# Mixture-of-experts layer on one core: sums over partitions by TensorE in place of GpSimd, one-hots in pairs of token columns

## The chip, the core and the metric
One core of a Trainium2 chip runs the whole layer as one program. The metric is the device time of one execution in microseconds (us). Engines are TensorE (PE, with PEld for its weight loads), VectorE (DVE), ScalarE (ACT), GpSimd (POOL) and the DMA issuer SyncE (SP). They run side by side, each through its own list of instructions in order, and wait for each other by semaphores.

## The reference
```python
xf = ifft(fft(x.reshape(B,T,4,64), axis=1) * gate, axis=1).real   # gate: one number per channel, so this scales x
x_right = hamilton(xf, conj(normalize(q_right)))                  # quaternion products, linear in x
c = hamilton(normalize(cond), x_right).reshape(B, T, 256)
h = c @ W_in + b_in                                               # "z" below
probs = softmax(h @ W_gate + b_gate)                              # 8 experts
topv, topi = top_k(probs, 2); topv = topv / sum(topv)
mid = relu(einsum('nd,edh->neh', h, W1) + b1)                     # 256 -> 1024, per expert
eout = einsum('neh,ehd->ned', mid, W2) + b2                       # 1024 -> 256
out = x + (sum over the 2 chosen experts of topv * eout) @ W_out + b_out
```
There are 4096 tokens of 256 channels, in float32. Only the two chosen experts of a token have to be worked out.

## The kernel before, in words
**Front.** The 4096 tokens are 32 columns of 128 tokens, handled as 16 pairs. TensorE transposes each pair of x (`x_pair`, L876), ScalarE copies it to `xt_sb` (L477). The whole conditioning and `W_in` are folded into one matrix `weff`, and the gate into `wg`, so that `logits_pair` (L885) and `z_pair` (L895, L898) are plain products of the transposed x. ScalarE copies z out of PSUM (L489) and squares it for its norm (L495), GpSimd stores it to DRAM (`z_by_token`, L397). VectorE picks the two experts of each token, counts tokens per expert, and gives each (token, choice) a slot: experts are put in an order by their counts, and each expert's slots are padded to a multiple of 256. The list "which token sits in which slot" is made by a product of one-hot matrices: VectorE writes `ohb` (row in a tile, 128 x 32 per choice k) and `oha` (tile column, 78 x 32, twice), L749 to L754, and TensorE multiplies them, one matmul for each of the 32 token columns and each k (`rows_of_slots`, L907, 64 matmuls).

**Tiles.** There are `NTILE` = 39 tiles of 256 slots. For tile a, GpSimd gathers its z rows by indirect DMA (`gather`, L428), TensorE transposes them (`rows_t`, L964, called "row transposes of tile a" below), ScalarE and VectorE split them into a high and a low half in float16 (`rows_high` L536, `rows_low` L794), TensorE runs the first layer (L983 to L985, 48 matmuls), ScalarE scales and clips (L549), VectorE splits again (L815, L817), TensorE runs the second layer (L998, 48 matmuls), VectorE finishes y (L805), and GpSimd scatters it (`scatter`, L435). TensorE's order is: first layer of a, row transposes of a+1, second layer of a-1. An expert has at least `GT` = 4 tiles; t = a % 4.

**Weights.** Those of the next expert come in while the current one is worked on. SP loads them (L321, L324), ScalarE squares them with a sum along each partition (L499, L504, in t = 0), GpSimd sums over the partitions (`norms`, L393, in t = 0) to get the norm, VectorE turns it into a power of two (`powers`, L662 to L664, in t = 1), GpSimd works out the scales of that expert (`table`, L411 to L421, in t = 1), and ScalarE and VectorE split the weights in four quarters (`piece`: L511 and L671, two in t = 2 and two in t = 3). A maximum over the partitions (L403) gives the scale of z.

**Order of GpSimd in the tile loop**, by hand:
```python
if a + 2 < NTILE: pool.wait_ge(s_tp, a + 1); gather(a + 2)
if a: scatter(a - 1)
j = a // GT + 1
if j < E and a % GT == 0: norms(j)
if j < E and a % GT == 1: table(j)
```
**End.** After the last tile the two choices of each token are loaded, mixed, transposed and multiplied with `W_out` (L1028, L1038).

## Time and profile before
| what | value |
| --- | --- |
| median of 3 runs | 677.98 us (672.96 to 685.27) |
| profiled execution | 670.79 us, its span 669.1 us |
| PE busy in the span | 578.9 us (87%) |
| DVE, ACT, POOL busy | 360.3, 298.0, 240.7 us |
| mean granted clock of PE | 0.918 of full speed |

The span is the time from the first to the last instruction of the profiled execution. All rows below come from that one execution, so differences are reckoned against its 670.79 us. A clock of 1.00 is TensorE's level of 2.4 GHz, 0.50 its level of 1.2 GHz.

### The profile page before, as it was taken

How to read it: one execution, taken by the hardware profiler on the slowest of the kernel's cores; microseconds unless marked ns; L12 is line 12 of the kernel's file. 1: busy time of each engine (PE TensorE's matmuls, PEld its weight loads, DVE VectorE, ACT ScalarE, POOL GpSimd, SP SyncE). 2: the span in 40 equal slices, each digit the busy share in tenths (PEclk: the TensorE clock that was granted, in tenths of full speed). 3: DMA queues.
4: the chain of work that ended last, by engine and by line, in shares of the span. 5: the costliest groups of instructions: out<-in, count | busy, mean ns of one | idle time of the engine just before them, and what ended most of it. 6: DMA issues, size and time to landing. Idle time of an engine off the chain costs nothing.

```text
span 669.1 us, 14435 instructions
## 1 busy us (share of the span) xinstructions
PE 578.9 (87%) x4527; PEld 493.5 (74%) x4528; DVE 360.3 (54%) x712; ACT 298.0 (45%) x534; POOL 240.7 (36%) x299
## 2 busy tenths in 40 slices
PE   3999993698996997996997898899799999992886
PEld 2996562486895886886886787687689898981665
DVE  5457404346556556556456357357455555542754
ACT  2404533445545555455455365366334343521443
POOL 4003112334345344344434425525524242317700
PEclk9959887789998998999899899899799999996799
DMA  6305215102412412412412402400111111148585
GB/s 189 105 1 206 101 47 181 32 30 98 120 48 88 127 40 93 126 40 90 129 36 82 134 32 87 139 25 32 63 48 49 47 57 40 49 143 280 169 271 189
DMA packets 40355, 64.64 MB, mean 97 GB/s; under 512 B 5943, under 2 KB 28156, under 8 KB 40316
## 3 DMA queue, kind: packets, MB, share of 16 engines
q1 hardware_dynamic: 31548, 39.51, 18.2%
q0 software_dynamic: 8768, 24.65, 11.4%
q8 instruction: 19, 0.31, 0.2%
q14 instruction: 20, 0.16, 0.1%
HBM read 45.53 MB, written 18.61 MB: 96 GB/s over the span
## 4 chain that ended last, share of the span: by engine, by line
PE 49%; issue 21%; POOL 14%; DMA 8%; DVE 4%; ACT 1%; SPq 1%; POOLq 1%; DVEq 0%; ACTq 0%
PE bank L998 19%; PE bank L898 5%; PE bank L983 4%; PE bank L985 4%; PE bank L984 4%; POOL region L428 4%; DMA region<-z_by_token,src 3%; PE bank L885 3%; POOL y_by_choice L435 3%; PE bank L907 3%; PE bank L964 2%; DMA w1s<-y_by_choice 2%; DMA w1s<-in_x 2%; POOL w1s L461 2%; PE bank L1028 1%
## 5 line engine op out<-in xcount | busy, mean ns | idle before, releaser
L549 ACT ACTIVATE region<-bank,b1p,cbits 128x256 f32<-128x256 f32 x312 | 157.0, 561 | 203.2 <-PE bank L985 143.9
L998 PE MATMUL bank<-w2s,region 128*128 x1872 | 218.8, 279 | 0.1
L998 PEld LDWEIGHTS bank<-w2s,region 128*128 128x128 f16 x1872 | 186.6, 100 | 27.0 <-issue 2.0
L983 PE MATMUL bank<-region,w1s 128*128 128x256 f16 x624 | 172.3, 276 | 3.6 <-DVE region L794 3.6
L984 PE MATMUL bank<-region,w1s 128*128 128x256 f16 x624 | 172.1, 276 | 0.0
L985 PE MATMUL bank<-region,w1s 128*128 128x256 f16 x624 | 172.0, 276 | 0.0
L435 POOL DMA_INDIRECT y_by_choice<-region,dst x78 | 80.8, 1036 | 171.3 <-DVE region L805 155.2
L815 DVE CAST region<-region 128x512 f16<-128x512 f32 x156 | 68.5, 439 | 114.3 <-ACT region L549 88.5
L817 DVE TENSOR_TENSOR region<-region 128x512 f16<-128x512 f32 x156 | 108.6, 696 | 5.4
L428 POOL DMA_INDIRECT region<-z_by_token,src x78 | 80.6, 1034 | 23.3 <-issue 22.2
L964 PE MATMUL bank<-ident,region 128*128 128x128 f32 x156 | 27.6, 306 | 50.1 <-DMA region<-z_by_token,src 50.1
L983 PEld LDWEIGHTS bank<-region,w1s 128*128 x624 | 61.8, 99 | 12.0 <-issue 4.2
L985 PEld LDWEIGHTS bank<-region,w1s 128*128 x624 | 61.8, 99 | 7.8
L984 PEld LDWEIGHTS bank<-region,w1s 128*128 x624 | 61.8, 99 | 7.7
L805 DVE SCALAR_TENSOR_TENSOR region<-bank,cbits,b2b 128x256 f32<-128x256 f32 x78 | 34.1, 479 | 48.4 <-PE bank L998 48.4
L964 PEld LDWEIGHTS bank<-ident,region 128*128 128x128 f32 x156 | 20.2, 156 | 53.1 <-DMA region<-z_by_token,src 52.7
L794 DVE SCALAR_TENSOR_TENSOR region<-bank,sx,region 128x512 f16<-128x512 f32 x39 | 29.1, 746 | 41.4 <-ACT region L536 41.4
L536 ACT ACTIVATE region<-bank,sx 128x512 f16<-128x512 f32 x39 | 26.9, 689 | 47.8 <-PE bank L964 29.4
L397 POOL DMA_DIRECT2D z_by_token<-w1s x16 | 12.5, 780 | 80.3 <-ACT w1s L489 80.3
L898 PE MATMUL bank<-w1s,w2s 128*128 128x256 f32 x128 | 37.2, 441 | 0.0
L850 DVE SCALAR_TENSOR_TENSOR w1s<-w1s,route 128x256 f32<-128x256 f32 x32 | 23.1, 766 | 19.2 <-ACT w1s L578 19.2
L898 PEld LDWEIGHTS bank<-w1s,w2s 128*128 128x128 f32 x128 | 26.7, 219 | 8.2 <-issue 4.5
(183 smaller groups left out, 488.0 us busy)
## 6 DMA issues: line engine op xcount, KB each, us to landing
region<-in_L_ffn_W SPq DMA_DIRECT2D x16, 1024.0 KB
w1s<-y_by_choice SPq DMA_DIRECT2D x16, 512.0 KB, 4.3
w1s<-in_x SPq DMA_DIRECT2D x8, 512.0 KB, 7.1
z_by_token<-w1s POOLq DMA_DIRECT2D x16, 256.0 KB, 2.7
w1s<-in_x SPq DMA_DIRECT2D x4, 1024.0 KB
out<-w1s SPq DMA_DIRECT2D x16, 256.0 KB, 2.6
region<-z_by_token,src POOLq DMA_INDIRECT x78
y_by_choice<-region,dst POOLq DMA_INDIRECT x78
```

Of the source, the lines that this page charges most:

```text
L428: g.indirect_dma_start(out=gx[:, a % 2, h, :], out_offset=None, in_=zbuf, in_offset=bass.IndirectOffsetOnAxis(ap=at, axis=0)).then_inc(s_g ...
L435: g.indirect_dma_start(out=ybuf, out_offset=bass.IndirectOffsetOnAxis(ap=at, axis=0), in_=ysb[:, a % 2, h, :], in_offset=None).then_inc(s_ ...
L549: m = s.activation(midf[:, b, c * TS:(c + 1) * TS], FB[b][:, c * TS:(c + 1) * TS], ACT.Relu, bias=b1p[:, bass.ds(r, 1), f:f + 1].rearrange ...
L805: last = v.scalar_tensor_tensor(ysb[:, par, h, :], YB[par][:, h * D:(h + 1) * D], cbits[:, 1, 1, bass.ds(r, 1)].bitcast(f32), b2b[:, bass. ...
L815: v.tensor_copy(mids[:, par, 0, b, :], midf[:, b, :]).then_inc(s_mh, 1)
L817: v.tensor_tensor(mids[:, par, 1, b, :], midf[:, b, :], mids[:, par, 0, b, :], ALU.subtract).then_inc(s_mq, 1)
L898: last = mm(bank[i % 4][:, t * D:(t + 1) * D], xt_sb[:, i, t, k, :], weff[:, k, :], start=False, stop=(k == KD - 1), skip_group_check=True)
L964: last = tr(XB[par][:, k * TS + h * P:k * TS + (h + 1) * P], gx[:, par, h, k * P:(k + 1) * P], ident[:])
L983: mm(o, w, xs[:, par, 0, k, :], start=(k == 0), stop=False)
L984: mm(o, w, xs[:, par, 1, k, :], start=False, stop=False)
L985: last = mm(o, w1_at(e, 1, k, 2 * b + c), xs[:, par, 0, k, :], start=False, stop=(k == KD - 1))
L998: last = mm(YB[par][:, h * D:(h + 1) * D], mids[:, par, l, b, c * TS + h * P:c * TS + (h + 1) * P], w2_at(e, w, f), start=(f == 0 and l == ...
```

## The change
1. The three kinds of sums over partitions leave GpSimd. The sum of squares of the weights becomes a matmul with a matrix of ones (`norms` on PE), after the first layer of each t = 1 tile, written to two columns of a transpose bank; VectorE copies it out in `powers`. The maximum for z becomes a transpose, a reduction on VectorE and a matmul. PE waits for `powers` in t = 2, and for the split weights (`s_wl`) in t = 0 of every expert.
2. The one-hots are laid out as (pair of token columns, entry, column in the pair): entries that a matmul reads one after the other lie 4 bytes apart. Before they lay 64 bytes apart.
3. The PSUM banks of the front are dealt out anew: transposes have two banks (`TB`), logits two (`LB`), z four (`ZB`) of their own. The product of the one-hots goes behind z pairs 8 and 11 (before 10 and 13).
4. ScalarE squares expert 0's weights two pairs earlier, and splits them after all z pairs; VectorE splits them after the exponents (`s_ho`).
5. The loop over experts covers 6 rather than 7 of them, the rest is written out.

```diff
-            def norms(j):
-                pool.wait_ge(s_sq1, j + 1)
-                pool.wait_ge(s_sq2, j + 1)
-                g.partition_all_reduce(wn[:, j, :], wss[:, j, :], P, RADD).then_inc(s_sp, 1)
...
-                if i == 11:
-                    norms(0)
-            pool.wait_ge(s_zn, 1)
-            g.partition_all_reduce(zmax[:, 1:2], zmax[:, 0:1], P, RMAX).then_inc(s_zm, 1)
...
-                if j < E and a % GT == 0:
-                    norms(j)
...
-                if i >= 12:
-                    piece(0, i - 12)
             z_squares(NP - 1)
+            for i in range(4):
+                piece(0, i)
...
+            def powers(j, at):
                 dve.wait_ge(s_sp, j + 1)
+                link(v.tensor_copy(wn[:, j], at))
...
-                v.tensor_tensor(ohb[:, k], iota16[:], bc(slot16[:, 1, k, :].unsqueeze(1), [P, P, NT]),
-                                ALU.is_equal).then_inc(s_ohu, 1)
+                v.tensor_tensor(ohb[:, k], bc(iota16[:].unsqueeze(1), [P, NB, P, 2]),
+                                bc(u.unsqueeze(2), [P, NB, P, 2]), ALU.is_equal).then_inc(s_ohu, 1)
...
-            piece(0, 0)
-            piece(0, 1)
-            piece(0, 2)
             dve.wait_ge(s_zsq, NP)
             v.tensor_reduce(zmax[:, 0:1], zss[:], AX.X, ALU.max).then_inc(s_zn, 1)
-            piece(0, 3)
+            dve.wait_ge(s_zt1, 1)
+            v.tensor_reduce(ztop[:], LB[0][0:1, 0:P], AX.X, ALU.max).then_inc(s_zt2, 1)
             dve.wait_ge(s_zm, 1)
+            link(v.tensor_copy(zmax[:, 1:2], LB[0][:, 0:1]))
...
+            for i in range(4):
+                piece(0, i)
...
-                    last = mm(bank[7][:, 0:2 * NA], ohb[:, k, :, t], oha[:, k, :, :, t],
+                    last = mm(bank[7][:, 0:2 * NA], ohb[:, k, t // 2, :, t % 2], oha[:, k, t // 2, :, :, t % 2],
...
+            def norms(j, at):
+                pe.wait_ge(s_sq1, j + 1)
+                pe.wait_ge(s_sq2, j + 1)
+                mm(at, ones[:], wss[:], start=True, stop=True).then_inc(s_sp, 1)
...
-                if i == 10:
+                if i == 8:
                     rows_of_slots(0)
-                if i == 13:
+                if i == 11:
                     rows_of_slots(1)
+                    norms(0, TB[1][:, 0:2])
+            pe.wait_ge(s_zn, 1)
+            tr(LB[0][0:1, 0:P], zmax[:, 0:1], ident[:]).then_inc(s_zt1, 1)
+            pe.wait_ge(s_zt2, 1)
+            mm(LB[0][:, 0:1], ones[0:1, :], ztop[:], start=True, stop=True).then_inc(s_zm, 1)
...
-                if t == 0 and not isinstance(a, int):
+                if t == 0 and (not isinstance(a, int) or g < E):
                     pe.wait_ge(s_wl, g * 4 + 4)
                 first_layer(a, par, expert(a))
+                if t == 1 and (not isinstance(a, int) or g + 1 < E):
+                    norms(g + 1, XB[par][:, 0:2])
+                if t == 2 and (not isinstance(a, int) or g + 1 < E):
+                    pe.wait_ge(s_s, g + 2)
```

The order of GpSimd at the table of expert 0 and the tiles behind it, first before (`wn<-wss` is the sum over partitions; ISA rows are control instructions):
```order
L411 CAST h<-hw 128x2 [waits powers_ready]
L412 ISA
L412 TENSOR_SCALAR kk<-h,hf 128x1 [waits pool_chain]
...
L421 ISA [waits pool_chain]
L421 TENSOR_TENSOR b1p<-bT,cbits 128x8
L428 DMA region<-z_by_token,src 128x256 x2
L428 DMA region<-z_by_token,src 128x256 [waits rows_transposed]
L428 DMA region<-z_by_token,src 128x256
L393 ISA
L393 ISA wn<-wss 128x2 [waits w2_squared,w1_squared]
```
and after:
```order
L402 CAST h<-hw 128x2 [waits powers_ready]
L403 TENSOR_SCALAR kk<-h,hf 128x1 [waits pool_chain]
...
L412 ISA [waits pool_chain]
L412 TENSOR_TENSOR b1p<-bT,cbits 128x8
L419 DMA region<-z_by_token,src 128x256 x2
L419 DMA region<-z_by_token,src 128x256 [waits rows_transposed]
L419 DMA region<-z_by_token,src 128x256
```
The sum with its ISA row is gone, and so is the ISA row ahead of the table's first TENSOR_SCALAR.

TensorE behind the second half of the z pairs, before:
```order
L907 MATMUL bank7<-region 128x156 [waits column_onehots_ready,row_onehots_ready]
L907 MATMUL bank7<-region 128x156 x31
L895 MATMUL bank2<-w1s,ones3 128x512 [waits z_copied]
L898 MATMUL bank2<-w1s,w2s 128x256 x4
L895 MATMUL bank3<-w1s,ones3 128x512 [waits z_copied]
L898 MATMUL bank3<-w1s,w2s 128x256 x4
L964 MATMUL bank2<-ident,region 128x128 [waits rows_gathered0]
```
and after:
```order
L904 MATMUL bank7<-region 128x156 [waits column_onehots_ready,row_onehots_ready]
L904 MATMUL bank7<-region 128x156 x31
L940 MATMUL bank3<-wss,ones 128x2 [waits w2_squared,w1_squared]
...
L892 MATMUL bank5<-w1s,ones3 128x512 [waits z_copied]
L895 MATMUL bank5<-w1s,w2s 128x256 x4
L962 MATMUL bank6<-ident,zmax 1x128 [waits z_norm_ready]
L964 MATMUL bank6<-ztop,ones 128x1 [waits z_norm_top_ready]
L972 MATMUL bank2<-ident,region 128x128 [waits rows_gathered0]
```
Four z pairs rather than two now stand behind the second set of one-hot products, the weights' sum stands ahead of them, and the two matmuls of z's maximum behind them.

VectorE ahead of the first tile, before:
```order
L671 SCALAR_TENSOR_TENSOR w1s<-region,s,w1s 128x1024 [waits weights_high] x2
L671 SCALAR_TENSOR_TENSOR w2s<-region,s,w2s 128x1024 [waits weights_high]
L783 TENSOR_REDUCE zmax<-zss 128x1 [waits z_squared]
L671 SCALAR_TENSOR_TENSOR w2s<-region,s,w2s 128x1024 [waits weights_high]
L786 TENSOR_SCALAR ho<-zmax 128x1 [waits z_norm_max_ready]
```
and after:
```order
L775 TENSOR_REDUCE zmax<-zss 128x1 [waits z_squared]
L777 TENSOR_REDUCE ztop<-bank 1x1 [waits z_norm_transposed]
L779 COPY zmax<-bank 128x1 [waits z_norm_max_product]
...
L663 SCALAR_TENSOR_TENSOR w1s<-region,s,w1s 128x1024 [waits weights_high,exponents_ready]
L663 SCALAR_TENSOR_TENSOR w1s<-region,s,w1s 128x1024 [waits weights_high]
L663 SCALAR_TENSOR_TENSOR w2s<-region,s,w2s 128x1024 [waits weights_high] x2
```
The four quarters of expert 0's weights moved behind the chain that gives the scale of z.

## Rows read from the trace of the kernel before

**Rows 1.** Busy time by stretch (us): PE, PEld, DVE, ACT, POOL, granted clock, DMA share, GB/s
```profile
140.10:472.50 332.40, 295.76 (x2603) 260.18 (x2601) 192.56 (x337) 170.13 (x287) 138.76 (x178) 0.94 0.25 81
472.50:583.40 110.90, 110.90 (x1002) 99.13 (x1003) 61.23 (x108) 47.26 (x90) 41.58 (x41) 0.99 0.17 51
```
**Rows 2.** Who waited for whom (us in total, times, longest), and GpSimd's last instructions
```profile
POOL kk L412 <- issue: 56.7, 8, 7.7
...
PE bank L964 <- DMA region<-z_by_token,src: 50.1, 9, 11.3
...
609.94 21.28 POOL L461 TENSOR_TENSOR w1s<-w1s,boutb 128x512 f32<-128x512 f32 x16 [1.58 <-DMA w1s<-in_x]
```
**Rows 3.** Timeline of GpSimd, tiles 4 to 6: start, duration, instruction, idle before
```profile
193.10 0.41 POOL L393 PARTITION_ALL_REDUCE wn<-wss  x1 [5.90 <-issue]
...
198.73 0.20 POOL L411 CAST h<-hw 128x2 f32<-128x2 int32 x1
206.35 0.87 POOL L412 TENSOR_SCALAR kk<-h,hf 128x1 f32<-128x1 f32 x1 [7.42 <-issue]
...
213.63 0.95 POOL L428 DMA_INDIRECT region<-z_by_token,src  x1 [0.30 <-issue]
```
**Rows 4.** Chain that ended last: start, us, what (tiles 8 and 31 to 38)
```profile
216.38 1.11 PE bank L964 x4
217.56 6.36 PE bank L998 x48
...
506.98 0.44 PE bank L964 x4
...
583.39 0.44 PE bank L964 x4
583.83 5.24 PE bank L998 x48
```
**Rows 5.** Timeline of PE, row transposes of tiles 1, 2, 5 and 7
```profile
129.83 0.66 PE L964 MATMUL bank<-ident,region 128*128 128x128 f32 x4 [2.24 <-DMA region<-z_by_token,src]
...
140.09 0.60 PE L964 MATMUL bank<-ident,region 128*128 128x128 f32 x4
...
177.74 0.60 PE L964 MATMUL bank<-ident,region 128*128 128x128 f32 x4
...
199.57 0.60 PE L964 MATMUL bank<-ident,region 128*128 128x128 f32 x4
```
**Rows 6.** Timeline of DVE, behind those of tile 7, and of tile 36
```profile
204.56 2.47 DVE L671 SCALAR_TENSOR_TENSOR w1s<-region,s,w1s 128x1024 f16<-128x1024 f32 x2
...
565.81 0.75 DVE L794 SCALAR_TENSOR_TENSOR region<-bank,sx,region 128x512 f16<-128x512 f32 x1
```
**Rows 7.** Timeline of ACT, end of the weights' squares in tile 4
```profile
185.24 0.20 ACT L504 ACTIVATION_READ_ACCUMULATOR w2s<-region 128x1 f32 x1
```
**Rows 8.** Chain that ended last, first one-hot products and the z pairs behind
```profile
74.01 8.84 PE bank L907 x32
...
83.39 3.44 PE bank L898 x8
...
87.15 1.92 PE bank L898 x8
```
**Rows 9.** Busy time inside the first one-hot products, columns as in rows 1
```profile
76.00:78.00 2.00, 2.00 (x9) 1.06 (x8) 0.00 (x0) 0.75 (x3) 0.72 (x1) 1.00 0.15 53
...
80.00:82.00 2.00, 2.00 (x9) 1.08 (x8) 0.00 (x0) 0.00 (x0) 0.00 (x0) 0.50 0.00 0
```
**Rows 10.** Timeline of DVE, last one-hot instruction of either choice
```profile
66.14 0.86 DVE L754 TENSOR_SCALAR region<-w2s,pid 128x2496 f16<-128x2496 f16 x1
...
72.11 0.86 DVE L754 TENSOR_SCALAR region<-w2s,pid 128x2496 f16<-128x2496 f16 x1
```
**Rows 11.** Timeline of PE, last z pair and row transposes of tile 0
```profile
104.26 1.99 PE L898 MATMUL bank<-w1s,w2s 128*128 128x256 f32 x8
117.56 1.12 PE L964 MATMUL bank<-ident,region 128*128 128x128 f32 x4 [11.30 <-DMA region<-z_by_token,src]
```

More of the change, by code:

```diff
@@ L16 @@
 from contextlib import ExitStack
-RMAX, RADD = bass.bass_isa.ReduceOp.max, bass.bass_isa.ReduceOp.add
 def moe_program(nc, x, cond, q_right, gate, W_in, b_in, W_gate, b_gate, W1, b1, W2, b2, W_out, b_out, out):
@@ L57, in moe_program @@
         YB = [bank[i] for i in (4, 5)]
-        LB = [bank[i] for i in (0, 1, 6, 7)]
+        LB = [bank[i] for i in (6, 7)]
+        TB = [bank[i] for i in (2, 3)]
+        ZB = [bank[i] for i in (0, 1, 4, 5)]
         w1s = sb("w1s", [P, E, 2, KD, F], f16)
@@ L281, in tiles @@
                 step(a, a % 2, 0, a)
-            with eng.Fori(1, E) as g:
+            with eng.Fori(1, E - 1) as g:
                 for t in range(GT):
                     step(g * GT + t, t % 2, g, t)
-            for a in range(E * GT, NTILE):
+            for a in range((E - 1) * GT, NTILE):
                 step(a, a % 2, a // GT, a % GT)
@@ L511, in piece @@
                 s.activation(high, raw, ACT.Copy, scale=scale).then_inc(s_wh, 1)
+            for i in range(AHEAD):
+                copy_xt(i)
             for i in range(NP):
-                copy_xt(i)
-                if i == 12:
-                    exp(0)
-            for g in range(1, LG):
-                exp(g)
+                if i + AHEAD < NP:
+                    copy_xt(i + AHEAD)
+                if i in (5, 9, 13):
+                    exp((i - 5) // 4)
+            exp(LG - 1)
             for i in range(NP):
@@ L695, in _ @@
                 dve.wait_ge(s_lgp, LT // 2 * (g + 1))
[L696 removed]
+                link(v.tensor_tensor(lg[:, t], LB[g % 2][:, 0:LT * E].rearrange("p (t e) -> p t e", e=E), bc(bg[:].unsqueeze(1), T3), ALU.add))
                 link(v.tensor_reduce(mx[:, 0, t], lg[:, t], AX.X, ALU.max))
@@ L766, in _ @@
             link(v.tensor_scalar(hbr[:, 2, :], hbr[:, 0, :], -1.0, 76.0, ALU.mult, ALU.add))
-            powers(0)
+            powers(0, TB[1][:, 0:2])
             dve.wait_ge(s_ohp, K)
@@ L822, in tile @@
                     if a % GT == 1:
-                        powers(j + 1)
+                        powers(j + 1, XB[par][:, 0:2])
                     if a % GT >= 2:
```

78 lines of the change are left out of this document (41 added, 37 removed).

## The prediction
> **What bounds the kernel now.** I read the busy time by stretch first, since the mean hides two different regimes. From 472.5 to 583.4 us PE is busy all the time at clock 0.99; from 140.1 to 472.5 it is busy 295.76 of 332.40 us at 0.94 [rows 1]. Tiles are the same work in both, so the second stretch shows what a tile costs undisturbed: the row transposes of tiles 31 and 38 start at 506.98 and 583.39, seven tiles apart, which is 10.916 us a tile [rows 4]. Between the row transposes of tile 2 (140.09) and of tile 28 (472.46, the edge of the first stretch) lie 26 tiles, 283.8 us at that rate, but 332.4 went by: 48.6 us lost, in seven places, one per expert.
>
> The list of waits names the place: PE waits 50.1 us in 9 waits at L964 for gathered rows, and GpSimd sits 56.7 us in 8 idles ahead of L412, released by nothing but issue [rows 2]. GpSimd's timeline joins the two: the sum over partitions takes 0.41 us, but 5.90 us pass idle ahead of it; the table's first TENSOR_SCALAR comes 7.42 us after the cast ahead of it, and the second gather of tile 8 is issued at 213.63 [rows 3]. Tile 8's row transposes then start at 216.38, at the lower clock: they take 1.11 us instead of 0.44, and the second layer behind them 6.36 instead of 5.24 [rows 4]. Before the tiles PE is the bound too: one unbroken row of work on it up to the last z pair, which ends at 106.25 [rows 11], and the 64 one-hot matmuls stand in it.
>
> **The change part by part.**
>
> *Code loading on GpSimd.* Every table has a sum over partitions between it and the last one, so its idle can't be told from a mere pause by the tables alone. Two things speak for the sum as the cause: GpSimd's additions near the end start 1.58 us after their releaser, though ten tiles with their indirect DMAs lie between them and the last table [rows 2], and in the order after, the ISA row ahead of the table's first TENSOR_SCALAR is gone together with the sum's own. I take it that both idles are loads of code that push each other out, and that they go together. GpSimd's 5.9 us ahead of the sum were mostly hidden, I think: the scatter next in its order waits for VectorE's y anyway. The 7.4 us were not. Without them the second gather of tile 8 is issued at 206.2; landing took 2.75 us (213.63 to 216.38), so the rows are there at 208.9, and PE wants them at 199.57 + 10.92 = 210.5 [rows 3 to 5]. Slack 1.6 us: the wait at L964 goes, and with it the drop of the clock. What is late next is PE itself.
>
> *The tiles in the sum.* From tile 2's row transposes (140.09) to tile 38's (583.39) took 443.3 us [rows 4, 5]. At the undisturbed rate 36 tiles take 393.0. Two things are added. Seven matmuls with ones sit on PE's path, in float32 like the transposes, of which one takes 0.44/4 = 0.11 us [rows 4]; with two passes and a weight load that nothing overlaps I put 0.3 us on each, 2.1 in all (bounds 0.1 and 0.5 each). And the wait on the split weights before the first layer in t = 0 had cover so far, the late rows. Undisturbed, PE reaches it 0.44 + 5.24 = 5.7 us after the row transposes [rows 4]. VectorE's last quarters end how long after them? In tile 6, where nothing was late, two quarters ended at 207.03, which is 7.5 us after tile 7's transposes [rows 5, 6]. In the undisturbed stretch `rows_low` starts 4.3 us after the transposes of tile 36 (561.5, two tiles of 10.92 back from 583.39), and two quarters behind its 0.65 us would end after 7.4. So PE waits about 1.7 us; I take 1.5 for each of the seven later experts, since ScalarE was now and then earlier, 10.5 in all. Bounds: 0, and 2.4. A wait this short need not cost clock: that is the unknown with the most weight, bounded below. Sum: 393.0 + 2.1 + 10.5 = 405.6, so 37.7 less than 443.3.
>
> *Waits that PE takes on.* The sum in t = 1 stands after the first layer of tile 4g+1, 10.9 us after that tile's transposes. Squares of the weights ended at 185.44, 7.7 us after tile 5's at 177.74 [rows 5, 7]. Slack 3.2 us, cost nothing; were it gone, the next transposes and a second layer queue behind it, one for one. `powers` runs on VectorE in t = 1 and PE asks for it a tile later: nothing.
>
> *One-hot products.* 32 of them take 8.84 us, 276 ns each [rows 8], and as many start in 2 us at clock 1.00 as at 0.50, nine [rows 9]. So it is not the multiplier that sets their rate but the fetch of operands 64 bytes apart. With 4 bytes apart, the nearest row is L998, float16 too, 5.24 us for 48 or 109 ns with 256 columns against 156 here [rows 4]. Bounds: 156/256 of that, 2.1 us for 32, and no change, 8.84. I take 109 ns, 3.5 us: the weight load is as long in both. Two sets give 10.7 us. The Trainium skill, SBUF — State Buffer, section on two separate sides, says that reads which cross into a new 16-byte line each time pay a penalty, and that two hits in a line are enough for the full rate; by it 4 bytes apart, four hits a line, would run at full rate. The rows agree as far as they go, and the lower bound would be its sum.
>
> *Clock behind them.* The z pair behind the first set took 3.44 us against 1.92 for the next one [rows 8], 1.5 us more at the lower clock; I take the same behind the second set. With shorter, denser products I count both as gained: 3.0 us. Together 13.7 us, less 0.3 for the weights' sum: the last z pair ends at 106.25 - 13.4 = 92.9.
>
> *Cover for the earlier place.* The product set k = 0 now starts behind pair 8, two pairs of 2.24 us ahead of 74.01 (86.83 to 89.07 is one), at 69.5 [rows 8]; its one-hots were ready at 67.0, those of k = 1 at 73.0, wanted at 69.5 + 3.5 + 3 x 2.24 = 79.7 [rows 10]. VectorE has the same elements in float16; I keep its times.
>
> *From the last z pair to tile 1.* Tile 0's row transposes came 11.3 us after the last z pair [rows 11], by copy, store, and gather from DRAM. That chain stays, so they come at 104.2, and it is the cover for the maximum of z, now four steps on PE and VectorE with a handover each. The four quarters behind it take 1.24 us each [rows 6]; if the maximum is there within 6 us of the last z pair, they end at 104, ahead of tile 0's rows. Each us later costs one, once. So nothing. Tile 1's waited another 2.24 us [rows 5] because its gather stood behind the table's 7.4; that goes. Tile 1's transposes move by 13.4 + 2.2 = 15.6.
>
> *Two PSUM banks for the transposes, the table and exp in other places, the loop of six.* A copy has a whole logits pair and the next transposes beside it, the list of instructions is the same, and the banks are the only new tie: nothing.
>
> **Sum:** 670.79 - 37.7 - 15.6 = 617.5. The median of the three runs lies 7.2 above the profiled execution. Part of this is, I think, late memory, for which the new kernel has slack at most places, so I add half: **620 us**, 8.5% faster than 677.98.
>
> **The rivals.**
> *A, the 7.4 us stay.* If the idle ahead of the table comes from the pause or from the indirect DMAs between tables, only the sum's 5.9 us go, which were hidden. The Trainium skill, GPSIMD Engine Reference, section on instruction dispatch, knows one such load, about 6 us at the first call of a freshly loaded kernel; that fits the 5.90, and it says nothing of a second when the old code is called again. The same page advises GpSimd for reductions along partitions, which speaks against the change. In rows: the loop keeps its 37.7 us, time 620 + 37.7 = 658. For it: no row shows a table without a sum. Against it: the missing ISA row and the additions at the end. 0.06.
> *B, the clock falls at the short waits of t = 0.* The lower clock cost tile 8 0.67 us in the transposes and 1.12 in the second layer [rows 4]; a drop that lasts 5 us in a first layer would cost 2.5. Seven times: 18 us, 638. For it: every long wait in the loop brought the clock down. Against it: tile 1's transposes, behind an idle of 2.24 us, took 0.66 us, so it was still up [rows 5]. 0.12.
> *C, the one-hot products keep their rate.* 13.7 us come back: 634. 0.10.
> *D, VectorE writes pairs at half rate.* A set takes 6.0 us (72.11 - 66.14) [rows 10], then 12. PE would wait 3.6 to 4.5 us at either set, 8 us: 628. For it: inner runs of two. Against: they are still float16 side by side. 0.08.
> *E, slower.* PE stands in order behind ScalarE and the weights' load in t = 1. If loading, now within 43.7 us an expert instead of 51 (332.4/26 x 4), made the squares late, every us over 3.2 would be paid seven times. It takes 3.2 + 53.3/7 = 10.8 us of lateness per expert to break even; at 13 it gives 620 + 7 x 9.8 = 689. Against it: the DMA share is 0.25 [rows 1]. 0.02.
> *Forecast:* 0.62.
>
> **How the numbers follow.** A measurement of this kernel can tell about 2% from no change. The range takes in D, C and B and the low bounds: no waits at t = 0 (-10.5), fetch at its low bound (-2.8), no surcharge (-3.6), which with a little for the clock in the first tiles gives 602 at the low end; B with its neighbours, 642, at the high. A and E, and two rivals together, are left out. Faster by over 2% (below 664) holds in all but E and a part of A: 0.95; within 2% 0.03; slower 0.02.
>
> **What would show it.** Right: no idle over 1 us ahead of the table's TENSOR_SCALAR; row transposes 43.7 to 46 us apart per four tiles; 32 one-hot products in 3 to 4 us; last z pair at 92 to 93. Wrong: row transposes that still wait for gathered rows (A), clock 0.5 at the start of an expert (B), one-hot products of 276 ns (C), PE idle ahead of them (D), PE idle at the sum in t = 1 (E). The prediction fails most easily in the wait for split weights, which no row before shows.

## The result, and the profile of the changed kernel

The changed kernel takes 647.38 us (median of four, 644.68 to 657.87) where the kernel before takes 681.18 (672.96 to 685.27) beside it: ratio 0.957, 95% interval 0.948 to 0.966. It is faster, as forecast, but 27 us slower than the 620 predicted and outside the range of 602 to 642. Medians here and below are over all runs of a kernel, ratios over those in the faster of the two states that its executions show, which leaves few runs and wide intervals in the fourth group.

The page of the profiled execution (649.58 us, span 647.8):

```profile
span 647.8 us, 14423 instructions
PEclk9755996899898999999899999899999999996899
```

By the starts of the row transposes (L972) of tiles 0, 2 and 38, with the predicted span of 615.8 (617.5 less the 1.7 outside it), and beside them the same kernel in a later run (e9, below):

| stretch, us | predicted | this profile | e9 |
|---|---|---|---|
| start to tile 0 | 104.2 | 108.89 | 109.76 |
| tile 0 to tile 2 | 20.3 | 20.70 | 20.72 |
| tile 2 to tile 38 | 405.6 | 433.20 | 404.27 |
| tile 38 to the end | 85.7 | 85.1 | 86.1 |
| span | 615.8 | 647.8 | 620.8 |

27.6 of the missing 32 us lie in the loop. The first place to look is GpSimd's timeline ahead of a table, where [rows 3] had 7.42 us of idle:

```profile
139.28 0.46 POOL L402 CAST h<-hw 128x2 f32<-128x2 int32 x1
139.85 0.75 POOL L403 TENSOR_SCALAR kk<-h,hf 128x1 f32<-128x1 f32 x1
```

That idle is gone. What PE waits for instead, from 129 to 470 us (us in total, times, longest):

```profile
PE bank L991 <- issue: 15.3, 6, 3.8
PE bank L972 <- DMA region<-z_by_token,src: 3.9, 4, 1.5
PE bank L991 <- DVE w2s L663: 2.9, 1, 2.9
```

The waits for gathered rows, 50.1 us in the whole trace before [rows 2] and 36.6 of them between tiles 2 and 38, have shrunk to 3.9 there, and a new wait stands in front of the first layer (L991) once per expert, 18.2 us in seven waits. The chain of waits at the first of them, tile 3 to tile 4:

```profile
151.51 0.54 PE bank L993
152.34 0.30 issue
152.64 0.56 ACT region L540
153.19 1.80 another core or an unknown queue
...
155.65 0.50 ACT region L540
156.17 0.44 DVE region L811
156.64 0.69 DVE region L813
157.33 0.66 DVE region L790
157.99 2.40 DVE w2s L663 x2
160.39 1.09 issue
161.48 0.39 PE bank L991
161.87 0.21 PE bank L992
```

PE's last product of tile 3's first layer ends at 151.62, yet ScalarE's last relu of that tile is released at 154.99 (153.19 + 1.80, by something that the chain can't name) and starts at 155.12; VectorE's two quarters of the split weights queue behind it and end at 160.39. PE idles, and the products after the wait are 0.21 us apart instead of 0.11: the granted clock is 0.50 from 160.6 us on, 1.2 GHz, for 6.8 us. In the front, PE's timeline:

```profile
22.76 1.09 PE L872 MATMUL bank<-ident,w1s 128*128 128x128 f32 x8
24.20 1.09 PE L872 MATMUL bank<-ident,w1s 128*128 128x128 f32 x4 [0.34 <-ACT w2s L466]
25.08 1.72 PE L884 MATMUL bank<-wg,w2s 128*128 128x8 f32 x8
...
42.25 15.37 PE L884 MATMUL bank<-wg,w2s 128*128 128x8 f32 x72
57.55 0.60 PE L892 MATMUL bank<-w1s,ones 3*128 3x512 bf16 x1
...
79.81 2.43 PE L904 MATMUL bank<-region 128*128 128x156 f16 x32
88.80 2.43 PE L904 MATMUL bank<-region 128*128 128x156 f16 x32
91.06 0.32 PE L940 MATMUL bank<-wss,ones 128*128 128x2 f32 x2
98.35 1.99 PE L895 MATMUL bank<-w1s,w2s 128*128 128x256 f32 x8
102.66 0.37 PE L962 MATMUL bank<-ident,zmax 128*1 128x128 f32 x1 [2.31 <-DVE zmax L775]
103.40 0.58 PE L964 MATMUL bank<-ztop,ones 1*128 1x1 f32 x2 [0.37 <-DVE ztop L777]
```

Eight products of the logits take 1.72 us here and took 0.96 in the trace before, whose clock held until 35 us; so the first z pair starts at 57.55 and not at 46.24. The one-hot products are down from 8.84 us [rows 8] to 2.43, or 71 ns from one to the next.

### The profile page after: what moved, and what is told of

Same layout as the page of the kernel before. It is cut to its first block, busy times and chain, and to the rows that moved or that the text cites. A ratio compares the mean times of both kernels' runs of the same rounds, so it can differ in the third digit from the quotient of the medians.

```text
span 647.8 us, 14423 instructions
## 1 busy us (share of the span) xinstructions
PE 573.0 (88%) x4546; PEld 495.8 (77%) x4547; DVE 360.8 (56%) x722; ACT 298.7 (46%) x534; POOL 245.3 (38%) x290
## 4 chain that ended last, share of the span: by engine, by line
PE 73%; DVE 7%; issue 5%; DMA 5%; ACT 2%; POOL 2%; another core or an unknown queue 2%; SPq 1%; ACTq 0%; DVEq 0%; POOLq 0%
PE bank L1006 25%; PE bank L993 10%; PE bank L991 10%; PE bank L992 10%; PE bank L895 5%; PE bank L884 4%; DMA w1s<-y_by_choice 3%; PE bank L972 2%; DVE w2s L663 2%; PE bank L872 2%; PE bank L1039 2%; ACT region L540 1%; DVE w1s L846 1%; DMA region<-z_by_token,src 1%
## 5 line engine op out<-in xcount | busy, mean ns | idle before, releaser
L1006 PE MATMUL bank<-w2s,region 128*128 x1872 | 212.6, 274 | 2.3 <-issue 2.2
L1006 PEld LDWEIGHTS bank<-w2s,region 128*128 128x128 f16 x1872 | 183.1, 98 | 26.1 <-issue 4.7
L991 PE MATMUL bank<-region,w1s 128*128 128x256 f16 x624 | 174.8, 280 | 22.7 <-issue 15.3
L992 PE MATMUL bank<-region,w1s 128*128 128x256 f16 x624 | 174.9, 280 | 0.0
L993 PE MATMUL bank<-region,w1s 128*128 128x256 f16 x624 | 174.9, 280 | 0.0
L419 POOL DMA_INDIRECT region<-z_by_token,src x78 | 78.7, 1009 | 27.6 <-issue 22.7
L991 PEld LDWEIGHTS bank<-region,w1s 128*128 x624 | 62.8, 101 | 34.3 <-issue 25.3
L993 PEld LDWEIGHTS bank<-region,w1s 128*128 x624 | 62.7, 100 | 8.7
L992 PEld LDWEIGHTS bank<-region,w1s 128*128 x624 | 62.7, 100 | 8.5
L972 PE MATMUL bank<-ident,region 128*128 128x128 f32 x156 | 24.7, 282 | 11.5 <-DMA region<-z_by_token,src 8.8
L895 PE MATMUL bank<-w1s,w2s 128*128 128x256 f32 x128 | 33.7, 408 | 0.0
L1039 PE MATMUL bank<-wout,w1s 128*128 128x256 f32 x128 | 31.6, 393 | 0.0
L569 ACT ACTIVATE w1s<-w1s,route 128x256 f32<-128x256 f32 x32 | 14.5, 500 | 35.2 <-DMA w1s<-y_by_choice 35.2
L1049 PE MATMUL bank<-ident,w1s 128*128 128x128 f32 x64 | 11.2, 302 | 20.6 <-DVE w1s L846 20.6
```

The source lines that it names most:

```text
L419: g.indirect_dma_start(out=gx[:, a % 2, h, :], out_offset=None, in_=zbuf, in_offset=bass.IndirectOffsetOnAxis(ap=at, axis=0)).then_inc(s_g ...
L895: last = mm(ZB[i % 4][:, t * D:(t + 1) * D], xt_sb[:, i, t, k, :], weff[:, k, :], start=False, stop=(k == KD - 1), skip_group_check=True)
L972: last = tr(XB[par][:, k * TS + h * P:k * TS + (h + 1) * P], gx[:, par, h, k * P:(k + 1) * P], ident[:])
L991: mm(o, w, xs[:, par, 0, k, :], start=(k == 0), stop=False)
L992: mm(o, w, xs[:, par, 1, k, :], start=False, stop=False)
L993: last = mm(o, w1_at(e, 1, k, 2 * b + c), xs[:, par, 0, k, :], start=False, stop=(k == KD - 1))
```

## The experiments

The runs fall into the first one, of the result, and four groups after it; a group shares a chip and its runs of the kernel before (the expectations say "call" for a group). "2 to 38" is the distance of the row transposes of these tiles in the trace. "Late" says whether PE's signals to ScalarE come late (e5).

| run | median us | ratio, 95% | late | tile 0 | 2 to 38 |
|---|---|---|---|---|---|
| before (the result) | 681.18 | | yes | 117.56 | 443.14 |
| changed (the result) | 647.38 | 0.957 [0.948, 0.966] | yes | 108.89 | 433.20 |
| e1 four banks | 625.27 | 0.914 [0.906, 0.921] | no | 115.39 | 403.65 |
| e2 half wait | 621.88 | 0.909 [0.901, 0.917] | no | 114.27 | 402.58 |
| e3 both | 616.71 | 0.901 [0.894, 0.907] | no | 105.73 | 404.71 |
| e4 unused sum | 671.68, one run | | no | 112.63 | 451.32 |
| e5 changed | 654.25 | 0.960 [0.952, 0.967] | yes | 109.11 | 433.07 |
| e6 z between logits | 648.85 | 0.949 [0.941, 0.956] | yes | 100.27 | 438.81 |
| e7 strided one-hots | 680.03 | 0.997 [0.993, 1.001] | yes | 132.43 | 439.54 |
| e8 loop sums only | 673.64 | 0.987 [0.980, 0.994] | yes | 120.89 | 439.91 |
| e9 changed | 622.84 | 0.915 [0.910, 0.920] | no | 109.76 | 404.27 |
| e10 half wait | 621.00 | 0.911 [0.906, 0.916] | no | 111.04 | 402.94 |
| e11 dense z, half wait | 612.10 | 0.897 [0.890, 0.903] | no | 101.33 | 403.57 |
| e12 direct rows | 616.80 | 0.906 [0.900, 0.911] | no | 108.05 | 401.00 |
| e13 changed | 647.22 | 0.951 [0.921, 0.981] | yes | 108.47 | 431.59 |
| e14 half wait | 625.30 | 0.926 [0.912, 0.939] | yes | 108.27 | 406.92 |
| e15 direct rows | 617.08 | 0.913 [0.903, 0.924] | no | 107.31 | 400.76 |
| e16 before | 674.09, one run | | yes | 119.48 | 445.66 |

### First group: front and wait

The theory was that the idle on ScalarE's copies at 24.20 cost the front its clock, and the wait for all four split weights the loop its 28 us. e1 gives the transposes of the tokens four banks again; e2 makes PE wait at t = 0 for half of the split weights only; e3 has both; e4 puts a sum that nobody uses back on GpSimd.

```diff
-        TB = [bank[i] for i in (2, 3)]
+        TB = [bank[i] for i in (2, 3, 4, 5)]
```


> The changed kernel with four PSUM banks for the transposes of x again (banks 2 to 5; two of them are also banks of z pairs, which come later). Theory: with two banks TensorE waits for ScalarE's copy at the eighth pair (0.34 us idle at 24.2 us), its clock falls to 1.2 GHz there and stays down through all logits, so the first z pair starts at 57.6 instead of 46.3 us. With four banks it starts at about 46.5, and the time falls by 11 us against the changed kernel. Rival: the fall of the clock has another cause (the logits themselves, or chance from one execution to the next); then the first z pair stays at 57 us and the time stays the same within 1 us.

```diff
-                    pe.wait_ge(s_wl, g * 4 + 4)
+                    pe.wait_ge(s_wl, g * 4 + 2)
                 first_layer(a, par, expert(a))
+                if t == 1 and (not isinstance(a, int) or g < E):
+                    pe.wait_ge(s_wl, g * 4 + 4)
```


> The changed kernel, but TensorE waits at the first tile of an expert only for the two quarters of W1, and for the two of W2 one tile later, ahead of the sum of squares. Theory: the wait for all four quarters costs the loop, each of seven times, about 3 us of idle and 3 us of lower clock in the first layer behind it; without it, the stretch from tile 2's row transposes to tile 38's falls from 433 to 405 to 410 us, the time by 23 to 28 us. Rival: ScalarE's lateness in tile 3 is the cause and reaches TensorE by another way, through rows_low of the next tile, about 1 us earlier than the quarters; then TensorE still idles 1 to 3 us per expert, the clock still falls, and the gain is 10 us or less.

> The two edits before together. If both theories hold and the places are apart, the gains add: 34 to 39 us against the changed kernel, 610 to 615 us for the profiled execution. By the rivals it is between 0 and 10 us.

```diff
+            def extra(j):
+                pool.wait_ge(s_sq1, j + 1)
+                pool.wait_ge(s_sq2, j + 1)
+                g.partition_all_reduce(unused[:, j, :], idle_in[:], P, bass.bass_isa.ReduceOp.add).then_inc(s_un, 1)
...
+                if j < E and a % GT == 0:
+                    extra(j)
                 if j < E and a % GT == 1:
                     table(j)
```


> The changed kernel with one sum over partitions added on GpSimd in t = 0 of each expert, of a constant, into a tile that nobody reads. Theory (two loads of code that push each other out): 5 to 6 us idle ahead of each sum and about 7 us ahead of each table's first TENSOR_SCALAR come back, seven times, gathers become late again and the time rises by 10 to 20 us. Rival (the idle ahead of the table came from the pause between tables or from indirect DMAs, and something else in the change removed it): idle only ahead of the sum, none ahead of the table, time unchanged within 2 us.

e4 settles what brings the two idles. GpSimd's waits in it, 120 to 480 us:

```profile
POOL kk L412 <- issue: 50.4, 7, 7.8
POOL unused L398 <- issue: 36.8, 6, 6.5
```

Both idles are back, 6.1 us ahead of a sum and 7.2 ahead of a table, with a sum whose result no one reads; and 47 us are back in the loop (451.32 to 404.27 in e9), where 10 to 20 had been expected. That an idle is the loading of code stays an inference: no view shows a load. The rest did not go as expected. With four banks the clock fell earlier (22.5 us, on no wait for ScalarE), the z pairs began at 56.98, and the theory of the banks fell. Tile 0 isn't the same from trace to trace either: with the changed kernel's own front and gathers it stands between 108.27 (e14) and 114.27 us (e2), with four banks at 115.39 (e1) and 105.73 (e3), so a few us there in one trace show nothing; e6, e7 and e11 below lie outside. The loop took 402 to 405 us in e1, e2 and e3 alike, in e1 with the wait as it was: PE's waits at L991 came to 0.7 us there. Either each edit had cured it, or the group was another kind of run; so e2's loop of 402.58, close to what its theory had forecast, proves nothing yet, and e3, at 616.71, had no two gains to add.

### Second group: the circumstances or the kernel

e5 is the changed kernel again, e8 the kernel before with the loop's sums on TensorE and the waits and copies that go with them.

> The changed kernel as it is, once more, beside the kernel before and three other kernels on one chip. In its first profile the row transposes of tiles 2 and 38 lay 433.2 us apart, in the runs with four banks 404.6 us, although nothing in the loop differed. Theory 1, the loop's extra 28 us belong to the execution (ScalarE's relus were late there, with waits whose releaser is called remote) and not to the kernel: here the distance is 404 to 412 us, no remote waits of ScalarE, and the ratio to the kernel before 0.91 to 0.93. Rival, they belong to the kernel (the wait of TensorE for all four split weights at the first tile of an expert): 425 to 435 us again, the waits ahead of the first layer 2 to 3.8 us each, ratio 0.95 to 0.96.

```diff
                 logits_pair(i)
-
-            for i in range(NP):
+                if i % 4 == 0:
+                    z_pair(i // 4)
+
+            for i in range(4, NP):
                 z_pair(i)
...
-                if i == 8:
+                if i == 12:
                     rows_of_slots(0)
-                if i == 11:
+                if i == 15:
                     rows_of_slots(1)
```


> Of the 16 z pairs the first four stand behind logits pairs 0, 4, 8 and 12 (they need no bank to be freed), the rest of the order follows. Theory 1, the granted clock falls to 0.5 because the logits (products with 8 columns) and little else run for 30 us, and comes back with the z pairs: with z pairs between them it stays at 1.0 for part or all of the logits, which then end at about 49 us instead of 57.6 with four z pairs done; the one-hots, the last z pair and tile 0 come some 7 to 9 us earlier, 636 to 642 beside 647 or the like of the changed kernel in this call. Rival, the clock falls there whatever stands between them (it fell at 20.8 to 34.8 us in the six profiles so far): the logits end at about 65 us, one-hots come later by 7 us and the time grows by 5 to 8 us.

```diff
-        ohb = region[:, 0:K * P * NT // 2].bitcast(f16).rearrange("p (k b c q) -> p k b c q", k=K, c=P, q=2)
-        oha = region[:, 4096:4096 + K * NA * NT].bitcast(f16).rearrange("p (k b s c q) -> p k b s c q", k=K, s=2, c=NA,
+        ohb = region[:, 0:K * P * NT // 2].bitcast(f16).rearrange("p (k c b q) -> p k b c q", k=K, c=P, q=2)
+        oha = region[:, 4096:4096 + K * NA * NT].bitcast(f16).rearrange("p (k s c b q) -> p k b s c q", k=K, s=2, c=NA,
```


> The changed kernel with the one-hots laid out again as before (all tokens of one column together, 64 bytes from one weight element of a product to the next), written by the same VectorE instructions. Theory 1, the stride is what made a one-hot product 276 ns and pulled the clock down behind it: 32 products take 8.8 us again instead of 2.26, the granted clock falls for some 4 us behind them, and the time is 13 to 18 us longer than that of the changed kernel in this call. Rival, the products were slow for another reason (new weights each time, nothing to overlap): they stay at 71 ns and the time within 2 us; VectorE's writing may take a few us more in both.

```diff
-                if j < E and a % GT == 0:
-                    norms(j)
...
+                if at is not None:
+                    link(v.tensor_copy(wn[:, j], at))
...
-                        powers(j + 1)
+                        powers(j + 1, XB[par][:, 0:2])
...
-                if t == 0 and not isinstance(a, int):
+                if t == 0 and (not isinstance(a, int) or 0 < g < E):
                     pe.wait_ge(s_wl, g * 4 + 4)
                 first_layer(a, par, expert(a))
+                if t == 1 and (not isinstance(a, int) or g + 1 < E):
+                    pe.wait_ge(s_sq1, g + 2)
+                    pe.wait_ge(s_sq2, g + 2)
+                    mm(XB[par][:, 0:2], ones[:], wss[:, bass.ds(g + 1, 1), :].rearrange("p e n -> p (e n)"), start=True,
+                       stop=True).then_inc(s_sp, 1)
+                if t == 2 and (not isinstance(a, int) or g + 1 < E):
+                    pe.wait_ge(s_s, g + 2)
```


> The kernel before with one part of the change alone: in the loop the sums over partitions are a TensorE product in the second tile of each expert, not GpSimd's; front, one-hots, z-norm maximum and expert 0 are as before. The prediction's own term for this is 443.3 to 405.6 us between the row transposes of tiles 2 and 38, so 37.7 us. Theory 1 (two code loads of GpSimd per expert were the whole loss, and the wait for split weights is rare): 36 to 41 us less than the kernel before, ratio 0.94 to 0.95. Rival (the sum on TensorE makes the next expert's weights late): 10 to 20 us less, with waits of 2 to 4 us ahead of the first layer of each expert.

e5 repeats the first profile's loop to 0.2 us. By its numbers the rival was right and the theory of one unlucky execution fell. Yet all four kernels of this group, e8 among them, which is an edit of the kernel before, show what all four of the first group lacked. ScalarE's timeline in tile 3 of the changed kernel of the result:

```profile
147.87 1.02 ACT L540 ACTIVATE region<-bank,b1p,cbits 128x256 f32<-128x256 f32 x2 [3.36 <-PE bank L993]
149.98 1.02 ACT L540 ACTIVATE region<-bank,b1p,cbits 128x256 f32<-128x256 f32 x2 [1.08 <-PE bank L993]
152.18 1.02 ACT L540 ACTIVATE region<-bank,b1p,cbits 128x256 f32<-128x256 f32 x2 [1.18 <-PE bank L993]
155.12 1.02 ACT L540 ACTIVATE region<-bank,b1p,cbits 128x256 f32<-128x256 f32 x2 [1.93 <-remote]
```

and of e9, the same program:

```profile
148.77 1.02 ACT L540 ACTIVATE region<-bank,b1p,cbits 128x256 f32<-128x256 f32 x2 [3.36 <-PE bank L993]
150.03 1.02 ACT L540 ACTIVATE region<-bank,b1p,cbits 128x256 f32<-128x256 f32 x2 [0.25 <-PE bank L993]
151.34 1.02 ACT L540 ACTIVATE region<-bank,b1p,cbits 128x256 f32<-128x256 f32 x2 [0.29 <-PE bank L993]
152.65 1.02 ACT L540 ACTIVATE region<-bank,b1p,cbits 128x256 f32<-128x256 f32 x2 [0.29 <-PE bank L993]
```

PE's matmuls stand 1.31 us a block apart in both; in e9 the relus follow at that step, in the other the second to fourth come 0.8, 1.7 and 3.3 us late. The event of the semaphore that PE raises at the end of a block is itself on record late, at 154.99 for the last block, 3.4 us behind the product that ended it at 151.62; the profile, finding no instruction that ended near the event, calls the releaser remote. e8 gained 3.2 us in the loop (439.91 to 443.14) and not 37.7: GpSimd's idle ahead of the table is gone from it, and PE waits 22.6 us ahead of its first layer (L983) instead, 2.9 to 3.5 each time. These are the waits that the rival named, but it gave 10 to 20 us less, and at 0.987 the kernel as a whole is within 2% of the one before.

e7 carries the one-hots: 32 products took 9.05 us, 278 ns from one to the next, and the z pair behind them 3.43 instead of 1.99. Tile 0 came 23.3 us later than in e5: 13.2 by the products, the rest by half-clock z pairs, by VectorE's own writing (3.66 for 2.29 us) and by a wait for gathered rows of 9.84 for 4.86. In all e7 took 25.8 us more than e5, where 13 to 18 had been expected. The layout is worth at least the 13.2 us of the products; the whole difference isn't its worth against the kernel before, since VectorE there wrote the same layout by other instructions. e6 brought tile 0 from 109.11 to 100.27 with the logits partly at the full clock, and then lost 5.7 of it in the loop; the ratios of e5 and e6 overlap, so that e6 is faster as a whole isn't shown. Busy time of PE, granted clock and DMA share in the front, e6 and then the changed kernel:

```profile
24.00:34.00 10.00, 10.00 (x59) 0.72 0.01 2
34.00:44.00 10.00, 10.00 (x74) 1.00 0.00 0
44.00:57.00 13.00, 11.84 (x67) 0.74 0.00 1
```
```profile
24.00:34.00 10.00, 9.80 (x48) 0.51 0.01 2
34.00:44.00 10.00, 10.00 (x50) 0.50 0.00 0
44.00:57.00 13.00, 13.00 (x62) 0.50 0.00 1
```

With only logits and transposes on PE the clock stayed at 0.50; with z pairs between them it came back. Why the clock of the kernel before held through the same gate products at 20 to 23 us isn't settled.

### Third group: signals on time

> The changed kernel as it is, for the third time, beside three others on one chip. In two calls it took 0.957 and 0.960 of the kernel before, and in its traces, as in those of all kernels of these two calls, TensorE's signals to ScalarE at the ends of blocks 2 and 3 of a tile's first layer came 1 to 2.3 us late (a block every 2.3 us and not every 1.31). In the call of the four-bank and half-wait kernels no kernel shows that. Theory 1, the lateness belongs to the chip or the call and costs the changed kernel some 28 us: it is in all four traces of this call or in none; with it the ratio is 0.955 to 0.965 and the row transposes of tiles 2 and 38 lie 430 to 436 us apart, without it 0.91 to 0.925 and 404 to 412 us. Rival, it belongs to the changed kernel alone and the edits of the other call took it away: this kernel has it and the half-wait kernel of this call has not.

> The kernel that waits for only two of the four split weights of an expert ahead of its first tile and for the other two after the first layer of the second tile, a second time. Theory 1, where the signals come late the wait at the first tile is what turns lateness into time (the chain of waits in the changed kernel: late relu of block 3, VectorE, the fourth split weight at 160.39, TensorE at 161.48, then a stretch at half clock): with late signals this kernel loses 0.5 to 1.5 us per expert where the changed one loses some 4 us, 15 to 25 us less than the changed kernel of this call; without late signals 0 to 5 us less. Rival, the lateness itself costs the time and not the wait: within 5 us of the changed kernel in both cases.

Over the half-wait kernel, e11 has:

```diff
                 logits_pair(i)
-
-            for i in range(NP):
+                if i in (0, 8, 10, 12):
+                    z_pair((0, 8, 10, 12).index(i))
+
+            for i in range(4, NP):
                 z_pair(i)
```


> The half-wait kernel, and of the z pairs the first four stand behind logits pairs 0, 8, 10 and 12. With z pairs behind logits pairs 0, 4, 8 and 12 the granted clock came back at 29.7 us and held to 46.7 us, and tile 0 began at 100.3 and not at 109.1 us. Theory 1, dense products right where the transposes of the tokens have run out hold the clock up: it stays at 1.0 from about 30 us through the logits, which end with four z pairs done at 48 to 51 us, and tile 0 begins at 95 to 99 us; the whole is 9 to 14 us less than the half-wait kernel of this call. Rival, the clock falls again at 45 to 57 us all the same: tile 0 at 100 us, 6 to 9 us less.

```diff
-                    at = src[:, 1, a * H + h:a * H + h + 1]
-                    g.indirect_dma_start(out=gx[:, a % 2, h, :], out_offset=None, in_=zbuf,
-                                         in_offset=bass.IndirectOffsetOnAxis(ap=at, axis=0)).then_inc(s_g[a % 2], 16)
+                    row = (a * H + h) * P % N
+                    g.dma_start(gx[:, a % 2, h, :], zbuf[row:row + P, :]).then_inc(s_g[a % 2], 16)
...
-                    at = dst[:, a * H + h:a * H + h + 1]
-                    g.indirect_dma_start(out=ybuf, out_offset=bass.IndirectOffsetOnAxis(ap=at, axis=0),
-                                         in_=ysb[:, a % 2, h, :], in_offset=None).then_inc(s_sc[a % 2], 16)
+                    row = (a * H + h) * P
+                    g.dma_start(ybuf[row:row + P, :], ysb[:, a % 2, h, :]).then_inc(s_sc[a % 2], 16)
```


> The changed kernel with the gathers and scatters of the loop as plain transfers of 128 rows that lie together, from the same queue with the same semaphores; so tokens and slots aren't matched, and the output isn't the reference's. Theory 1, TensorE's late signals come from the indirect transfers (rows of 1 KB scattered over memory, their descriptors written by GpSimd): where the other kernels of this call show blocks 2.3 us apart, here they are 1.31 us apart and the time falls by 15 to 30 us. Rival, they have another cause (the chip, the load of the weights): blocks stay 2.3 us apart where the others' do, and the time is within 5 us. If no kernel of this call has late signals, this one tells only what the indirect form costs, within 5 us by both.

The unedited kernel took 622.84, 0.915 of the kernel before. Its waits, PE's and then ScalarE's, from 129 to 470 us:

```profile
PE bank L972 <- DMA region<-z_by_token,src: 5.5, 6, 1.6
...
PE bank L991 <- issue: 0.6, 1, 0.6
```
```profile
ACT region L540 <- PE bank L993: 113.7, 113, 5.6
ACT region L540 <- issue: 31.2, 8, 4.7
```

No remote releaser, and no wait for split weights to speak of, so the half wait had nothing to save (1.8 us). e11 is the fastest of all: tile 0 at 101.33, 9.7 us ahead of e10, total 8.9 less. Theory 1 had tile 0 at 95 to 99; the rival came nearer, and the clock averaged 0.86 from 44 to 57 us. e12 tells only the price of the indirect form here, 6.0 us.

### Fourth group: late signals again

> The changed kernel as it is, so that the call's kind is known. Either signals of TensorE come late (blocks 2 and 3 of a tile's first layer some 2.3 us after the one before): 645 to 655, ratio 0.955 to 0.965; or they come on time (1.31 us): 619 to 628, ratio 0.91 to 0.92. By the theory that the call sets it, nothing lies between.

> The half-wait kernel. With late signals, theory 1 (the wait for the fourth split weight at an expert's first tile turns them into time): 15 to 28 us less than the changed kernel of this call; rival (late signals cost the time by way of the rows of the next tile, which stand behind the same late relu): within 5 us of it. With signals on time both say 0 to 4 us less, as measured once (621.0 beside 622.8).

> The changed kernel with the loop's gathers and scatters as plain transfers of 128 neighbouring rows; tokens and slots aren't matched, and the output isn't the reference's. With late signals in this call, theory 1 (the indirect transfers cause them): blocks at 1.31 us here, 616 to 620, 28 us or so less than the changed kernel; rival (they come from something else): blocks at 2.3 us, within 10 us of it. With signals on time: 616.8 beside 622.8 as before, so 4 to 8 us less.

> The kernel before, for its trace beside the others of this call. Its own first trace had late signals (waits of ScalarE with a remote releaser: 16.3 us) and 443.3 us between the row transposes of tiles 2 and 38. Theory 1, late signals cost it little, as its tile 3 lay in GpSimd's idle time, without transfers, and the weights of the next expert were ready well ahead of the first tile: whichever kind this call is, the distance is 438 to 446 us. Rival, with signals on time it falls to 425 to 435 us.

This group had late signals, so the theories of e14 and e15 could be told from their rivals. e14 beside e13: PE's waits of e13 at L991 (14.9 + 3.6 us) are gone although ScalarE is as late as ever. Waits of e14, PE's and ScalarE's:

```profile
PE bank L991 <- DVE region L790: 1.4, 2, 0.7
```
```profile
ACT region L540 <- remote: 27.6, 18, 3.3
```

The wait is thus what turns late signals into time. The loop shrinks from 431.59 to 406.92 us and the time by 21.9 (639.2 to 652.4 in e13, 623.3 to 628.0 in e14). e15, in the same group, has relus at 148.48, 149.79 and 151.10, 1.31 us apart:

```profile
148.48 1.02 ACT L538 ACTIVATE region<-bank,b1p,cbits 128x256 f32<-128x256 f32 x2 [0.25 <-PE bank L991]
149.79 1.02 ACT L538 ACTIVATE region<-bank,b1p,cbits 128x256 f32<-128x256 f32 x2 [0.29 <-PE bank L991]
151.10 1.02 ACT L538 ACTIVATE region<-bank,b1p,cbits 128x256 f32<-128x256 f32 x2 [0.29 <-PE bank L991]
```

so in this group the signals came late only with indirect transfers under way. It is one kernel of one group, and what of the indirect form does it, the scattered rows or their preparation, wasn't taken apart.

The kernel before doesn't care: its median is 680.7 to 683.6 us in the groups with late signals and 681.8 and 684.9 in those without. e16 couldn't test its rival, which needed signals on time; it has the late signals too, and its loop took 445.66 us, as theory 1 had it. PE waited for rows behind the 7.4 us of GpSimd's idle anyway, in which no transfers went out, and in the trace before the relus of the tile ahead of a new expert come on time, 0.14 to 0.18 us after their block's last product. That this idle is the cover is argued from the traces, not tried.

## Why the prediction missed

*Code loads, both go together:* both idles went together, as forecast. None is left ahead of the table, and e4 brings both back. The Trainium skill, GPSIMD Engine Reference, section on instruction dispatch, knows one load, at the first call of a freshly loaded kernel; the trace shows an idle at each change between the two kinds of instruction, 7 us back and 6 us forth. The same page's advice, in its section on engine selection, to reduce along partitions on GpSimd is contradicted here: L940 takes 0.32 us for both passes, against 0.41 and the two idles.

*The tiles in the sum, 405.6:* this is the step that failed, in the term "1.5 for each of the seven later experts" of wait on the split weights, 10.5 us in all. Measured, the seven waits are 0.4 to 3.8 us each and 18.2 in all, and what rival B priced comes on top: the granted clock was 0.50 for 17.1 us in four stretches, which costs 8.5. That makes 26.7 of the 433.20 - 393.0 = 40.2 us over undisturbed tiles, where 12.6 had been given; 8.7 more is idle ahead of row transposes and second layers, and 4.8 the norm products and small pieces.

The term rested on a misread row. Two quarters ended 7.5 us after tile 7's transposes "in tile 6, where nothing was late", but ScalarE's relus of that tile were late in the trace before:

```profile
195.98 1.02 ACT L549 ACTIVATE region<-bank,b1p,cbits 128x256 f32<-128x256 f32 x2 [5.42 <-PE bank L985]
199.65 2.84 ACT L549 ACTIVATE region<-bank,b1p,cbits 128x256 f32<-128x256 f32 x6 [2.66 <-PE bank L985]
```

On time the second block would start 1.31 us after the first, at 197.29. So the 7.5 had lateness of another tile in it, and the lateness that the changed kernel would have ahead of each new expert was nowhere in the sum. There VectorE ends its last quarter 7.0 to 9.4 us after the transposes of the expert's first tile, in e9 4.9 to 5.6, and PE wants it after 5.7. With signals on time the same sum comes within 1.3 us (404.27), but not for its reason, so that is luck: hardly a wait for weights (0.6), instead 5.5 us for gathered rows in six places and the rest in small pieces. Late signals, which stood in the waits of ScalarE of the trace before (16.3 us by a remote releaser), were no rival at all, and the upper bound of 2.4 us a wait has no row beside it.

*Norm products, 0.3 us each:* right, 0.25 from the first pass at 91.06 to the next product at 91.31.

*The sum in t = 1 has slack 3.2:* held, no wait of PE there in any trace (rival E out).

*One-hots, 3.5 us for 32:* 2.43, better by 1.1 each, between the taken value and the low bound of 2.1. The Trainium skill, SBUF — State Buffer, section on two separate sides, on reads that cross into new 16-byte lines: e7 agrees, 278 ns against 71 for the same products. Rivals C and D are out.

*Clock behind them:* gained, as taken; e7 brings the dip back.

*"Two PSUM banks for the transposes, the table and exp in other places...: nothing":* wrong for the front as a whole. The clock fell at 24 us and not at 35, which moved the z pairs by 11.3 us. The last z pair ended at 100.34, where 92.9 was forecast: 11.3 late, 2.1 back from the one-hots, the rest in small pieces. That the banks did it is refuted by e1.

*From the last z pair to tile 1:* tile 0 came 8.5 us after the last z pair instead of the 11.3 kept, a small gain; the z maximum was over at 104, hidden as said, and tile 1 no longer waited.

So in the result: front +4.7, loop +27.6, tail and rest -0.3 us. Where signals come on time the kernel takes 622.8, and the forecast of 620 would have looked right by errors that cancel.

## What to carry to other kernels

When an idle stretch is to be removed, ask what it covers: here, as far as the traces tell, 7.4 us of GpSimd's standing still kept transfers out of the tile ahead of a new expert and its relus on time, and a wait on all four quarters of the next weights turned late relus into 4 us an expert once it was gone. Let an engine wait only for the part that it reads next (half of the weights, one line), and the time hardly depends on how late the rest is (the loop took 406.92 us with late signals, 402.58 and 402.94 without). Where TensorE's clock has fallen in the front, work that is independent and heavier, here the z pairs, may bring it back if it is moved between the lighter products.

## What was not expected of the hardware

PE's signals at the end of a block reach ScalarE late in some groups, up to 3.3 us in the tile shown, and not in others, in all kernels of a group that gather and scatter by index. Semaphore events on record in the traces:

```
late:     changed 4057, e5 3994, e6 4017, e7 4053, e8 4011, e13 4106, e14 4085, before 4385, e16 4397
on time:  e1 5696, e2 5706, e3 5704, e4 5717, e9 5703, e10 5712, e11 5699, e12 5714, e15 5713
```

Late traces of the changed kernel and its variants lack over a quarter of their events, without exception; e15, in a group of late signals, has them all. Most of what is missing belongs to transfers: of the events of the gathers' and scatters' semaphores 1181 are on record in the changed kernel's profile and 2500 in e9 and in e15. The Trainium skill, NOTIFIC — the notification-queue block, section 7.1 on overflow, says that the block which writes such records can hold up the engines that produce them. That would fit the lateness, though not by itself the missing records, and it would mean that the recording makes the lateness. The number of events alone isn't it, as e15 raises as many as e13. But every execution timed here was recorded, so no run can tell, nor what sets a group on one side or the other. The chip alone doesn't, if its number tells it apart: the first and the fourth group bear the same one.
